# A two-layer graph network on one core: the one-hots of the first stage read the node numbers from PSUM, and the destinations are stored positive

## The reference, cut to what matters

```python
agg = segment_sum(x[src], dst, N)                   # layer 0: plain sum over the edges
z = relu(((1 + eps) * x + agg) @ W1 + b1) @ W2 + b2
x1 = layernorm(x + batchnorm(z) + x)
sup = segment_sum(edge_weight * x1[dst], src, N)    # layer 1: the same edges, other way round, weighted
out = layernorm(x1 + relu(sup @ weight))
```

## Time and profile before

| | us |
|---|---|
| median of 3 runs | 4498.2 |
| lowest and highest | 4492.72 and 4502.33 |
| the profiled execution's own time | 4497.28 |
| its span, first to last instruction | 4495.5 |
| first stage: first gather, last gather, last matmul into a tile | 7.0, 2259.6, 2285.8 |
| second stage: first gather, last gather | 2452.1, 4466.8 |

### The profile page before, as it was taken

One profiled execution on the slowest core, in us unless ns is written; L12 is line 12 of the kernel. 1 busy time (PEld: TensorE's weight loads), 2 busy tenths in 40 slices (PEclk: granted clock), 3 DMA queues, 4 the chain that ended last, 5 costly groups with the idle time before them and its releaser, 6 DMA issues.

```text
span 4495.5 us, 70641 instructions
## 1 busy us (share of the span) xinstructions
PE 3471.4 (77%) x16131; PEld 2855.9 (64%) x16132; DVE 2613.0 (58%) x5752; ACT 438.8 (10%) x1160; POOL 3331.5 (74%) x3352
## 2 busy tenths in 40 slices
PE   4777877877877787787744887888888888888887
PEld 3666665666666566566633666666666666666665
DVE  6776877777777777677656343344344344443443
ACT  1000000000000000000034000000000000000001
POOL 7777777777777777777733777777777777777775
PEclk7988888888888888898865999999999999999999
DMA  5333333333333333333376334344434443444343
GB/s 147 109 109 112 109 111 108 114 112 109 111 110 112 108 110 111 109 113 110 103 244 220 113 113 119 115 119 119 119 114 119 119 119 115 119 119 119 114 120 101
DMA packets 297894, 539.36 MB, mean 120 GB/s; under 512 B 77802, under 2 KB 190302, under 8 KB 297838
## 3 DMA queue, kind: packets, MB, share of 16 engines
q0 software_dynamic: 159424, 434.52, 33.3%
q10 hardware_dynamic: 89348, 67.77, 4.9%
q1 hardware_dynamic: 49066, 36.39, 2.7%
HBM read 489.80 MB, written 46.88 MB: 119 GB/s over the span
## 4 chain that ended last, share of the span: by engine, by line
POOL 64%; issue 22%; PE 7%; DMA 3%; POOLq 1%; ACT 1%; DVE 1%; ACTq 0%; SPq 0%; DVEq 0%; PEldq 0%
POOL ring L548 32%; POOL ring L606 32%; PE ps L1278 4%; DMA ring<-in_x,idx 1%; PE ps L1368 1%; DMA x_dram<-ring 1%; PE ps L1496 1%; POOLq L617 1%; DMA z_dram<-z_pair 0%; DMA ring<-x_dram,idx 0%; ACT ring L1741 0%; PE ps L1348 0%; PE ps L1335 0%; POOLq L618 0%; PE ps L1288 0%
## 5 line engine op out<-in xcount | busy, mean ns | idle before, releaser
L548 POOL DMA_INDIRECT ring<-in_x,idx x1664 | 1746.0, 1049 | 510.5 <-issue 501.0
L606 POOL DMA_INDIRECT ring<-x_dram,idx x1612 | 1524.0, 945 | 518.0 <-issue 490.1
L1496 PE MATMUL ps<-ring,work 128*128 x6448 | 1519.5, 391 | 341.9 <-SPq L524 340.4
L1496 PEld LDWEIGHTS ps<-ring,work 128*128 128x128 f32 x6448 | 1217.4, 193 | 629.8 <-issue 475.9
L1149 DVE TENSOR_SCALAR work<-ps,dstT,wT 128x256 f32<-128x256 f32 x1612 | 742.2, 539 | 1133.4 <-PE ps L1496 1066.2
L1278 PE MATMUL ps<-ring,ones_sb 128*128 x3324 | 958.2, 439 | 359.1 <-SPq L456 280.8
L1278 PEld LDWEIGHTS ps<-ring,ones_sb 128*128 128x128 f32 x3324 | 711.1, 222 | 523.3 <-issue 412.4
L897 DVE SCALAR_TENSOR_TENSOR ones_sb<-dstT,tile_base,minus_iota 128x256 f32<-128x256 f32 (+1 forms) x294 | 316.8, 1105 | 264.9 <-issue 225.1
L1368 PEld LDWEIGHTS ps<-work 128*128 128x128 f32 x3384 | 429.6, 197 | 14.8
L1368 PE MATMUL ps<-work 128*128 128x128 f32 x3384 | 427.6, 279 | 0.0
L882 DVE TENSOR_TENSOR work<-ps,current 128x768 f32<-128x768 f32 x282 | 267.8, 950 | 9.9 <-PE ps L1368 9.9
(11 more groups left out here) (250 smaller groups left out, 2254.8 us busy)
## 6 DMA issues: line engine op xcount, KB each, us to landing
ring<-in_x,idx POOLq DMA_INDIRECT x1664
ring<-x_dram,idx POOLq DMA_INDIRECT x1612
z_dram<-z_pair ACTq DMA_DIRECT2D x49, 256.0 KB
ones_sb<-x_dram ACTq DMA_DIRECT2D x49, 256.0 KB
ring<-z_dram SPq DMA_DIRECT2D x24, 512.0 KB, 5.8
ring<-in_x SPq DMA_DIRECT2D x24, 512.0 KB, 7.2
x_dram<-ring ACTq DMA_DIRECT2D x24, 512.0 KB, 4.0
out<-ones_sb ACTq DMA_DIRECT2D x48, 256.0 KB
```

The costliest lines, as they stand in the source:

```text
L548: nc.gpsimd.indirect_dma_start(out=ring[:, q, c, :], out_offset=None, in_=x, in_offset=bass.IndirectOffsetOnAxis(ap=idx[:, q, c:c + 1], ax ...
L606: nc.gpsimd.indirect_dma_start(out=ring[:, q, c, :], out_offset=None, in_=x1_dram, in_offset=bass.IndirectOffsetOnAxis(ap=idx[:, q, c:c + ...
L1496: last = nc.tensor.matmul(to[:, t * D:(t + 1) * D], ones_of[:, b, c, t * P:(t + 1) * P], ring[:, ds((p + b) & (RING - 1), 1), c, :].rearra ...
```

## The change

The node numbers of the one-hots come from `p_iota` in PSUM instead of `minus_iota` in SBUF. The test becomes `p_iota + base == dstT`, so `dstT` has to hold the destinations with their own sign: ScalarE copies them out of PSUM without the factor -1, and the four other places that read them change their sign. `minus_iota` and the instruction that makes it go away, and two waits of TensorE count one less.

```diff
-            setup(nc.vector.tensor_scalar(minus_iota[:, :], iota_f[:, 0:P], -1.0, None, ALU.mult))
...
-                nc.vector.tensor_scalar(pad[:, :], dst_k, -float(BIG), None, ALU.is_le).then_inc(s_sort, 1)
+                nc.vector.tensor_scalar(pad[:, :], dst_k, float(BIG), None, ALU.is_ge).then_inc(s_sort, 1)
...
-                nc.vector.scalar_tensor_tensor(out=key[:, :], in0=dst_k, scalar=-float(BUCKET),
+                nc.vector.scalar_tensor_tensor(out=key[:, :], in0=dst_k, scalar=float(BUCKET),
...
                     return nc.vector.scalar_tensor_tensor(
                         out=to.rearrange("p b c n -> p (b c) n"),
-                        in0=dstT[:, ds(at, n), :].rearrange("p b c -> p (b c)").unsqueeze(2).to_broadcast([P, 2 * n, P]),
-                        scalar=base, in1=minus_iota[:, :].unsqueeze(1).to_broadcast([P, 2 * n, P]), op0=ALU.add, op1=ALU.is_equal)
+                        in0=p_iota.unsqueeze(1).to_broadcast([P, 2 * n, P]), scalar=base,
+                        in1=dstT[:, ds(at, n), :].rearrange("p b c -> p (b c)").unsqueeze(2).to_broadcast([P, 2 * n, P]),
+                        op0=ALU.add, op1=ALU.is_equal)
...
-            setup(nc.vector.tensor_tensor(selfT[:, :, :], srcT[:, 0:ROWS, :], dstT[:, :, :], ALU.add))
+            setup(nc.vector.tensor_tensor(selfT[:, :, :], srcT[:, 0:ROWS, :], dstT[:, :, :], ALU.subtract))
...
-            pe.wait_ge(s_setup, 10 + 2 * NB)
+            pe.wait_ge(s_setup, 9 + 2 * NB)
...
-            pe.wait_ge(s_setup, 10 + 2 * NB + 2)
+            pe.wait_ge(s_setup, 9 + 2 * NB + 2)
...
-                        nc.scalar.activation(to[:, b0 * P:(b0 + n) * P, c], ps[:, banks[n_bank % 4], 0:n * P], ACT.Copy,
-                                             scale=-1.0 if to is dstT else 1.0).then_inc(s_lists, 1)
+                        nc.scalar.activation(to[:, b0 * P:(b0 + n) * P, c], ps[:, banks[n_bank % 4], 0:n * P], ACT.Copy).then_inc(s_lists, 1)
```

More of the change, by code:

```diff
@@ L132, in gnn @@
         tile_base = sb("tile_base", [P, NT], f32)
-        minus_iota = sb("minus_iota", [P, P], f32)
         ranks_f = sb("ranks_f", [P, THIRDS + 1, NB1], f32)
```

## The result

| | before, us | after, us |
|---|---|---|
| median of 4 runs each | 4498.48 | 4382.89 |
| lowest and highest | 4492.72 and 4502.33 | 4380.47 and 4383.74 |
| span of the profiled execution | 4495.5 | 4378.6 |
| first stage: end of the last gather | 2259.6 | 2101.75 |
| first stage: last matmul into a tile | 2285.8 | 2168.5 |

The ratio of the times is 0.9743, with an interval of 0.9726 to 0.976: 116 us less, where 119 were predicted (4379 against 4382.89). All of it is won by the end of the first stage; from there both kernels take the same: 4495.5 - 2285.8 = 2209.7 us before, 4378.6 - 2168.5 = 2210.1 after.

What follows compares the result with a forecast made beforehand. First-stage gathers on GpSimd, held up by one-hots, bound the kernel; VectorE would take over. 105 us in the loop plus 14 at its end, 119, off the 4495.5 span gives 4376.5, median 4379 us; range 4350 to 4408.

Steps and rivals of the forecast that it cites:

- The stall and its cause: First-stage gathers: one-hots with two SBUF inputs hold them up; with one in PSUM, up to 166 us of GpSimd's time goes.
- VectorE takes over: First-stage loop: once gathers are not held, VectorE bounds with 1982 us against GpSimd's 1925; chance 78%.
- The margin to the gathers: First-stage loop, 100 to 2187 us: VectorE needs 1982 us, GpSimd without its stalls 1925.
- The first rival: First stage: the gathers stay the bound, so the gain is their 166 us and the time 4332; chance 6%.
- 105 us in the loop: VectorE waits that can go: 91.0 us at line 816, 9.9 at line 882, 4.0 at the one-hots.
- the idle time before the one-hots: VectorE in the loop: 213.8 us in 89 waits, filled by the sequencer's 2.71 us table load; it stays.
- 43.4 us throughout: Sign in the changed profile: every VectorE block in the loop lasts 43.4 us, as a block without lateness does.
- 14 us at the stage's end: End of the first stage: with all rows landed, tile 95 ends 14 us earlier relative to tile 94.
- The one-hots' own length: One-hot instructions on VectorE: 482 and 2352 ns as before; bounds 57 ns longer or 69 shorter, +16 or -19 us.
- TensorE as the bound: Rival, first-stage loop: TensorE's busy time grows by 15%, it needs 2058 us, time 4455, partly 4408 to 4455; chance 7%.
- No gather over 1.2 us in the loop: Sign in the changed profile: no first-stage loop gather exceeds 1.2 us, with line 548's mean near 946 ns.
- GpSimd waiting for room: Gathers running ahead of TensorE may wait for room in the ring at the end; this costs nothing.

Runs made afterwards that it cites:

- experiment 1: The changed kernel with the one-hots' node numbers read from SBUF again, the rest of the change kept: 4497.96 us, kernel before 4496.52, ratio 1.0004.
- experiment 2: The changed kernel with VectorE's table load for the next tile moved right behind a tile's one-hots: 4340.95 us, kernel before 4499.32, ratio 0.9649.
- experiment 3: The changed kernel with one more VectorE comparison in each block, into a tile nothing else reads: 4424.89 us, kernel before 4496.42, ratio 0.9849.
- run 1631: Not a run's number: "that run" is experiment 2's, the changed kernel with the table load moved, 4340.95 us; 1631 counts its gathers.
- experiment 6: The kernel before with the table load moved right behind the previous tile's one-hots, four sets on the slower chips: ratios 1.0056, 1.0015, 0.9981 and 0.9986.

## Why the prediction was right, point by point

- **The stall and its cause: right.** Gathers over one-hots are no longer held (1550.80 us for 1632), and experiment 1 brings it all back by one operand.
- **VectorE takes over: right.** The chain after, experiments 2 and 3 each show it. The margin to the gathers was put at 1982 - 1925 = 57 us in the loop; by experiment 2 it is 42 at the end of the stage. The first rival, the gathers as bound, was given 4332; with VectorE out of the way the kernel takes 4340.95. The difference of 9 is mostly what is left of held gathers: in that run 1631 of them take 1550.27 us over the stretch of the earlier trace rows, 7.3 more than at 0.946 each.
- **105 us in the loop: nearly right.** The one-hots of tile 94 start at 2083.84 and end at 2087.1 after, 2187.5 before: 100.4. The step that was mis-sized is the idle time before the one-hots, taken as unchanged. By the rows of VectorE's waits it was 213.8 / 89 = 2.40 us each and is 228.8 / 93 = 2.46, so 93 x 0.06 = 5 us. It lies before the one-hots of even tiles. Of tiles 6 to 92 the even ones have 3.55 us of it on the mean, 3.25 before (13 us in all; before the odd ones 7 us are gone). One of them:

```profile
1031.11 3.27 DVE L895 SCALAR_TENSOR_TENSOR ones_sb<-ps,tile_base,dstT 128x256 f32<-128x256 f32 x3 [3.79 <-issue]
1038.79 0.62 DVE L783 TENSOR_TENSOR ps<-ps,before_mask 128x432 f32<-128x432 f32 x1
...
1083.17 0.62 DVE L783 TENSOR_TENSOR ps<-ps,before_mask 128x432 f32<-128x432 f32 x1
```

  What fills it is the sequencer's load: for those even tiles it takes 3.01 us on the mean and took 2.71. Why it is longer now was not tried. "43.4 us throughout" was wrong too: this block takes 1083.17 - 1038.79 = 44.4. After the first one, four blocks take 41.0 to 41.5 us, the later ones 43.2 to 44.4. Before the change 43.4 was an ordinary block, but three of the later ones take 47 to 50 even with their wait at line 816 cut to 0.94, which makes a mean of 43.9 (43.7 after, by the same count). It did not hurt the sum, which went by the waits.
- **14 us at the stage's end: nearly right, 16.7.** Tile 95's last matmul stands 31.4 us behind the one-hots of tile 94 and not 48.1. The wait that hung on it (19.58 us in the earlier trace rows) is 9.35, and what follows moved along: TensorE's 21.75 us wait in the earlier trace rows is 21.53.

```profile
2118.73 3.27 DVE L895 SCALAR_TENSOR_TENSOR ones_sb<-ps,tile_base,dstT 128x256 f32<-128x256 f32 x3 [9.35 <-PE ps L1260]
```

```profile
2142.69 0.37 PE L1272 MATMUL ps<-zeros 1*128 1x257 bf16 x1 [21.53 <-ACT agg L1606]
...
2167.89 0.59 PE L1260 MATMUL ps<-x_pair,self_term 128*128 128x256 f32 x2
```

  The sum is 100.4 + 16.7 = 117.1 for 119. The two terms missed in opposite directions, by 4.5 and 2.6 us, so that the sum is closer than its terms is luck; the last tile was put near 2167 and ended at 2168.5, the second stage's first gather near 2333 and stood at 2335.4.
- **The one-hots' own length: right.** 482 and 2352 became 479 and 2351 ns. The bounds of 57 ns more and 69 less weren't needed. The 120 cycles of the Trainium skill ("VectorE: DVE Perf Modes", section on the TRN2 errata), against 58 in SBUF, would have added some 65 ns to each; no row here shows it, and the sum by them, 4397, was missed by 14 us.
- **TensorE as the bound: right to leave it.** In 100 to 2070 us it is busy for 1569.71 at a granted clock of 0.88 (0.86 before), and its largest wait is for one-hots.
- **"No gather over 1.2 us in the loop": wrong by six.** Five take 1.23 to 1.24 us and one, at 1917.79, takes 1.33. All six start inside line 788, another VectorE instruction that reads two things from SBUF. Such instructions hold gathers in both kernels; in the changed one lines 788 and 791 lengthen 38 gathers, by 5.8 us in all. Before the change nearly all of the excess stood at line 897 (115 gathers, 163.7 of 173.3 us, setup included); that the hold there kept the gathers in step with VectorE and away from the short instructions is argued, not shown.
- **GpSimd waiting for room: it hardly came.** There are 10.7 us in 33 waits, 5.5 in 18 before, but all except one are the usual 0.30 us; the one takes 0.99, at 2092.0 us. GpSimd's slack went into 40.6 us more of lead instead. With more work on VectorE (experiment 3) it does wait, 54.7 us in 53.

## What to carry to other kernels

Where GpSimd issues indirect gathers one after another, count how many start inside a VectorE instruction with two SBUF inputs. Here each such start costs what is left of that instruction less about 0.13 us, and one input moved to PSUM takes the cost away without making the instruction longer (479 ns for 482). Before you book the whole excess as gain, sum what the next engine needs: here VectorE could give 105 of the 166 us. Then look again, since the new bound has its own cheap spots: moving a 2.7 us register load was worth 42 us once the wait at the old line 816 was gone; that it was free behind this wait before is argued (experiment 6).

## What the hardware showed that was not expected

- **A gather is held by a one-hot with two SBUF inputs only if it starts inside it**, and then until about 0.82 us after the one-hot's end; one under way when the one-hot begins takes its usual 0.95 us (the first row of experiment 1's timeline). Not every start inside counts: in four traces with the numbers in SBUF (the kernel before and the three sets of runs of experiment 1) no gather is held that starts up to 0.094 us into a one-hot, nor one that starts within its last 0.12 us, and all that start from 0.105 us on with 0.147 us or more left are held. So, as an estimate from these rows, what VectorE runs some 0.1 us after the gather's start decides.
- **A plain tensor_tensor holds it too.** In the setup of the changed kernel, before the loop, the longest gather of all stands over line 926, which subtracts one SBUF tensor from another:

```profile
45.11 2.02 DVE L926 TENSOR_TENSOR selfT<-srcT,dstT 128x1792 f32<-128x1792 int32 x1
45.18 2.76 POOL L547 DMA_INDIRECT ring<-in_x,idx  x1 [0.30 <-issue]
```

  The Trainium skill ("SBUF — State Buffer", section on who interferes with whom) reports a probe in which tensor_tensor did not stall a DMA of GpSimd, and infers that making the descriptors of such a transfer needs the interface for writes, which tensor_tensor leaves free. The rows here disagree for an indirect gather: 2.76 us instead of 0.946, ending 0.82 us behind the instruction.
- **Two SBUF inputs are not the only way.** In the setup of the kernel before, a conversion of int32 to float32, with one SBUF input, holds a gather that began 0.48 us ahead of it, 1.70 us instead of 0.946:

```profile
8.46 1.70 POOL L548 DMA_INDIRECT ring<-in_x,idx  x1 [0.30 <-issue]
8.65 4.31 SPq L424 DMA_DIRECT2D ones_sb<-in_dst  x1
8.94 1.09 DVE L643 CAST ring<-ring 128x1792 f32<-128x1792 int32 x1 [7.80 <-DMA ring<-in_src]
```

  It ends 0.12 us behind the conversion (0.118 to 0.120 in five traces). Where a gather starts inside the same conversion, as in the changed kernel (at 8.44 us, 1.82 us long), it ends 0.82 us behind it. Which property of this instruction matters was not tried.
- **The same kernel takes 4496 to 4499 us on some chips and 5362 to 5443 on others**, at a granted clock of about 0.82 instead of 0.90 and with matmuls apart without a wait. An edit has to be timed against the kernel before on the same chip.
